# A decoder layer on one core: narrower score tiles, other head groups for the second attention, and three steps in another order

## The reference, cut to what matters

```
x = x + gla(layernorm(x))                 # stage a: gated linear attention, 16 heads, causal
x = x + xattn(layernorm(x), ctx)          # stage b: cross attention over 128 context rows
x = x + moe(layernorm(x))                 # 4 experts, top 2, capacity 512 tokens

gla:   S = S * exp(g) + k v^T ; o = q S   (per head, dk = 16, dv = 32)
       = for a block of 32 queries: scores = (q decayed)(k decayed)^T, masked, then times v
xattn: s = LN(q) LN(k)^T / sqrt(32); p = softmax(s); o = p v; out = o Wo
logits = layernorm(x) Wg                  # the router, 4 columns
```

## Time and profile before

| | us |
|---|---|
| runs | 1056.18, 1051.98, 1054.56 |
| median | 1054.56 |
| profiled execution, its own time | 1056.18 |
| its span, first to last instruction | 1054.4 |
| PE busy | 935.3 (89%) |
| DVE, POOL, ACT busy | 697.2, 493.9, 450.1 |

### The profile page before, as it was taken

The page is one execution under the profiler, slowest core; times in us unless marked ns, Lnnn a source line. Parts: engine busy times, 40 slices in busy tenths (PEclk is TensorE's granted clock), DMA queues, the critical chain, the costliest instruction groups (busy, mean ns, idle before and its releaser), DMA issues.

```text
span 1054.4 us, 19146 instructions
## 1 busy us (share of the span) xinstructions
PE 935.3 (89%) x7297; PEld 552.5 (52%) x7297; DVE 697.2 (66%) x1293; ACT 450.1 (43%) x754; POOL 493.9 (47%) x563
## 2 busy tenths in 40 slices
PE   3588999999999999999998763069999999999995
PEld 1445666667667666666665432024444444444342
DVE  6767787877887788878786435856555445446572
ACT  3444655665556655565565423112233323233210
POOL 1446676777777677767677520011070001003643
PEclk9788999999999999999999856569999999999998
DMA  9413000000000000000000005132335235235593
GB/s 288 132 51 127 4 17 17 4 17 17 14 17 3 17 14 17 2 17 17 14 2 14 12 11 197 52 119 81 118 85 182 96 119 161 82 117 171 175 245 129
DMA packets 40300, 78.39 MB, mean 74 GB/s; under 512 B 11378, under 2 KB 11650, under 8 KB 40258
## 3 DMA queue, kind: packets, MB, share of 16 engines
q1 hardware_dynamic: 35266, 63.13, 18.0%
q0 software_dynamic: 4992, 14.70, 5.1%
HBM read 64.16 MB, written 13.65 MB: 74 GB/s over the span
## 4 chain that ended last, share of the span: by engine, by line
PE 74%; DVE 7%; POOL 5%; issue 4%; DMA 4%; SPq 3%; ACT 2%; POOLq 0%; DVEq 0%; ACTq 0%
PE ps L1009 18%; PE ps L1010 17%; PE ps L1011 17%; PE ps L1015 6%; PE ps L1103 5%; PE ps L1195 3%; PE ps L1182 3%; POOL y_fetched L728 2%; PE ps L1206 2%; PE ps L1226 1%; POOL hrs L596 1%; DVE big L1678 1%; PE ps L1115 1%; SPq L473 1%; DMA y_fetched<-y_scratch,idx_get 1%
## 5 line engine op out<-in xcount | busy, mean ns | idle before, releaser
L596 POOL TENSOR_TENSOR hrs<-hve,neg_half 128x16 f32<-128x16 f32 x48 | 144.1, 3003 | 3.8
L982 ACT ACTIVATE big<-ps 128x512 f32<-128x512 f32 x64 | 38.2, 597 | 234.0 <-PE ps L1011 233.8
L1775 DVE TENSOR_SCALAR big<-big 128x512 f16<-128x512 f32 x64 | 27.7, 432 | 112.7 <-ACT big L982 112.7
L1009 PE MATMUL ps<-w2h,big 128*128 128x512 f16 x256 | 97.0, 379 | 2.7 <-DVE big L1367 2.7
L1009 PE MATMUL ps<-big,w1h 128*128 128x512 f16 x256 | 98.1, 383 | 1.4 <-DVE big L1367 1.4
L1010 PE MATMUL ps<-big,w1h 128*128 128x512 f16 x256 | 98.0, 383 | 0.0
L1011 PE MATMUL ps<-big,w1l 128*128 128x512 f16 x256 | 98.0, 383 | 0.0
L1011 PE MATMUL ps<-w2h,big 128*128 128x512 f16 x256 | 97.0, 379 | 0.0
L1010 PE MATMUL ps<-w2l,big 128*128 128x512 f16 x256 | 97.0, 379 | 0.0
L711 POOL DMA_INDIRECT big<-x_scratch,token_of x16 | 18.3, 1146 | 150.0 <-PE ps L1015 77.5
L728 POOL DMA_INDIRECT y_fetched<-y_scratch,idx_get x32 | 36.7, 1148 | 105.0 <-DMA y_scratch<-big 89.4
(11 more groups left out here) (305 smaller groups left out, 2498.8 us busy)
## 6 DMA issues: line engine op xcount, KB each, us to landing
wst<-in_w SPq DMA_DIRECT2D x28, 1024.0 KB, 5.2
x_scratch<-xn SPq DMA_DIRECT2D x16, 256.0 KB, 2.1
y_fetched<-in_w SPq DMA_DIRECT2D x4, 1024.0 KB, 13.7
out<-x_all SPq DMA_DIRECT2D x4, 1024.0 KB, 9.3
pr<-in_w_attn SPq DMA_DIRECT2D x3, 1024.0 KB, 9.1
x_all<-in_w_attn SPq DMA_DIRECT2D x3, 1024.0 KB, 11.7
x_all<-in_x SPq DMA_DIRECT2D x1, 3072.0 KB, 12.4
y_scratch<-big SPq DMA_DIRECT2D x3, 1024.0 KB, 6.1
```

Source lines behind the costliest of these rows:

```text
L596: pool.tensor_tensor(hrs[n][:, :], hve[n][:, :], neg_half[:, :], ALU.pow).then_inc(hdev[n], 1)
L982: act.activation(hg[f % 2], psum[f % 2][:, 512:1024], ACT.Gelu, scale=UN).then_inc(hg_r, 1)
L1009: nc.tensor.matmul(o, lh, rh, start=first, stop=False)
```

## The change

The score matmuls take exactly the width that their block needs. The four turns of b2 take two rows of heads and two columns each (`pv_heads`), so that turns 0 and 1 use only the half of the probabilities from round 0 and wait for that half alone; the values' matmuls follow the same grouping. On PE `a1_g` is one step, `b1_x` comes ahead of `b2_logits`. On ACT `x3_out` comes after the second layer norm's row and after `ctx_hi`, and `x2_hi` ahead of `logits_out`.

```diff
@@ ACT, body
                 on(s[1], kv_out)
-                on(s[3], x3_out)
                 on(s[1], row_norm, 1, xn2, xn2_r)
                 on(s[0], ctx_hi)
+                on(s[3], x3_out)
+                on(s[1], x2_hi)
                 on(s[3], logits_out)
-                on(s[1], x2_hi)
@@ PE, a2_scores
-                            w = max(KTW[i], 3 * BLK)
-                            o = psum[1][0:w, col:col + 256].rearrange(...)[:, :, i * BLK:(i + 1) * BLK]
-                            last = nc.tensor.matmul(o, kt[par][rw, c, KTO[i]:KTO[i] + w],
+                            o = psum[1][0:KTW[i], col:col + 256].rearrange(...)[:, :, i * BLK:(i + 1) * BLK]
+                            last = nc.tensor.matmul(o, kt[par][rw, c, KTO[i]:KTO[i] + KTW[i]],
                                                     qeo[par][rw, c * NBLK + i, :, :], start=True, stop=True)
@@ PE, b2
+            def pv_heads(g):
+                return [(2 * (g // 2) + i, 2 * (g % 2) + c) for c in range(2) for i in range(2)]
             def b2_turn(s, r):
-                for rnd in range(2):
-                    after(pe, pr_r[rnd], b)
+                after(pe, pr_r[r // 2], b)
...
-                for rr in range(4):
-                    last = nc.tensor.transpose(d0[:, rr * L:(rr + 1) * L], pg[:, rr * KC + r, :], ident[:, :])
+                for i, (rr, c) in enumerate(pv_heads(r)):
+                    last = nc.tensor.transpose(d0[:, i * L:(i + 1) * L], pg[:, rr * KC + c, :], ident[:, :])
             def b2_pv(s, r):
...
-                for rr in range(4):
-                    h = 4 * r + rr
-                    last = nc.tensor.matmul(d1[32 * rr:32 * rr + 32, r * L:(r + 1) * L], vx[par][:, h * DV:(h + 1) * DV],
-                                            pT[r % 2][:, rr, :], start=True, stop=True)
+                for i, (rr, c) in enumerate(pv_heads(r)):
+                    h = 4 * c + rr
+                    last = nc.tensor.matmul(d1[32 * rr:32 * rr + 32, c * L:(c + 1) * L], vx[par][:, h * DV:(h + 1) * DV],
+                                            pT[r % 2][:, i, :], start=True, stop=True)
@@ PE, body
                 on(s[3], b2_x3)
-                on(s[0], a1_g, range(KC // 2))
+                on(s[0], a1_g)
+                on(s[1], b1_x)
                 on(s[3], b2_logits)
-                on(s[0], a1_g, range(KC // 2, KC))
-                on(s[1], b1_x)
```

More of the change, by code:

```diff
@@ L1016, in turn, with rows @@
                 last.then_inc(done, 1)
-            def rows(ps, xh, xl, col, done, opens=True, ks=range(KC)):
-                for k in ks:
+            def rows(ps, xh, xl, col, done, opens=True):
+                for k in range(KC):
                     last = mm3(ps, xh[:, k, :], xl[:, k, :], wh[:, k, col:col + D], wl[:, k, col:col + D], opens and k == 0, k == KC - 1)
-                if k == KC - 1:
-                    last.then_inc(done, 1)
+                last.then_inc(done, 1)
             def second_kv():
@@ L1083, in a1_v, with a1_g @@
                 rows(a1, xth, xtl, C_V, v_ps)
-            def a1_g(s, ks):
+            def a1_g(s):
                 b, par, half = s
@@ L1088, in a1_g @@
                 after(pe, v_r, b)
-                rows(a1, xth, xtl, C_G, g_ps, ks=ks)
+                rows(a1, xth, xtl, C_G, g_ps)
             def a2_scores(s, rnd):
@@ L1100, in a2_scores @@
                             col = (r % 2) * 512 + c * 256
-                            w = max(KTW[i], 3 * BLK)
-                            o = psum[1][0:w, col:col + 256].rearrange("p (e t) -> p e t", e=2)[:, :, i * BLK:(i + 1) * BLK]
-                            last = nc.tensor.matmul(o, kt[par][rw, c, KTO[i]:KTO[i] + w],
+                            o = psum[1][0:KTW[i], col:col + 256].rearrange("p (e t) -> p e t", e=2)[:, :, i * BLK:(i + 1) * BLK]
+                            last = nc.tensor.matmul(o, kt[par][rw, c, KTO[i]:KTO[i] + KTW[i]],
                                                     qeo[par][rw, c * NBLK + i, :, :], start=True, stop=True)
```

## The result

The changed kernel takes 1095.56 us (median of 4 runs, 1094.20 to 1101.68) against 1054.94 us of the kernel before (4 runs, 1051.98 to 1056.18): a ratio of 1.0400, 95% interval 1.0355 to 1.0446, so 40.6 us slower. The forecast was 1086.6 us, 32 us slower, with a range up to 1098. Direction and range held; the size was 8.6 us short, and part of the time came by a way that the forecast doesn't name.

What follows compares the result with a forecast made beforehand. PE was taken to bound the loop, bodies 3 to 15. Widths 16.6, strips 12.8, half wait 0 and order 2.6 gave +32.0 us: 1086.6 us against the 1054.56 median; range for 8 in 10, 1072 to 1098.

Steps and rivals of the forecast that it cites:

- part 4: New order on PE and ACT: PE waits 0.3 us for x3T, 0.1 comes back; +2.6 us (0 to 5.2).
- the third rival: Ring of other engines bounds the loop, not PE; earlier x2h shortens bodies: -11, 1043.6 us; chance 0.03.
- the fourth: Rival for the whole kernel: what the change adds is hidden, time the same within 0.5%; chance 0.04.
- Part 1: Exact score widths: five more tile shape changes a round at 0.15 us, 0.23 saved; net +0.52 a round, +16.6 us.
- The first rival: Score rounds: changes between column widths within 32 rows don't drain; +8, 1062.6 us; chance 0.10.
- ten more waits put down to "issue" a body: Sign at the scores: PEld's count of waits put down to "issue" rises by some ten a body.
- Part 2: Values' matmuls in two strips instead of four: +0.21 us a step, four a sequence; +12.8 us (0 to 15).
- The changes of shape around it stay as they were: Value steps: assumed unchanged tile shape changes around each, so two more passes add +0.21 us to each step.
- The second rival: Value steps: four heads of `b2_pv` in two strips cost nothing more; +19.2, 1073.8 us; chance 0.10.
- Part 3: Turns waiting for half the probabilities: 3.8 us of slack in the loop, so nothing to gain; 0 us.
- just fits: Seam before the scores: `a1_g` ends at 317.54, xn2 at 317.36, so `b1_x` isn't delayed; 0.6 to spare before.
- is unchanged: PE between 314.95 and the scores at 318.88: same sum of instructions; only waits can change.

Runs made afterwards that it cites:

- the kernel with the blocks outside: Changed kernel with score loops turned round (query blocks outside, column halves inside), widths 128, 96, 64, 64: 1071.24 us, 1.0156 to the kernel before.
- the kernel with the strips: Kernel before with only the two-strip head groups and the wait for half of the probabilities: 1065.90 against 1060.44 us, 1.0055.
- the kernel with x3T first: Changed kernel with ACT's x3_out back ahead of the second layer norm's row, PE's order kept: 1091.47 us, 1.0343 to the kernel before.
- the first three experiments: Kernel before with one part each: exact score widths 1074.86 us, two-strip head groups 1065.90, new PE and ACT order 1068.27, against 1060.44.
- widths with strips: Changed kernel with the old order on PE and ACT, exact widths and head groups kept: 1078.47 against 1060.44 us, 1.0191.

## Why the forecast was right, and where it was not

**What bounds the kernel.** Right. The change of PE's busy time (+45 us) is about 2 us off the change of the span (+42.8), and the only wait for another engine that lengthened the body is the one for x3T, in part 4. By that the third rival falls (the ring of other engines): DVE's wait for x2h shrank from 2.91 to 2.11 us, and the body grew by the sum of PE's pieces. So does the fourth (hidden).

**Part 1, widths.** Right in mechanism, slightly long in size: 0.445 us a round instead of 0.52, because a change of shape from one width to another costs about 0.135 us and not 0.15. In 13 bodies that is 2.0 us less than forecast. The first rival (no drain between widths) is refuted by the round of 2.06 us. Shape by shape, PEld's loads did become shorter as forecast. Weight loads of the changed kernel from 150 to 187 (form, count, total us and mean ns of one, idle us before them):

```profile
L1101 PEld LDWEIGHTS ps<-qeo,kt 32*128 32x128 f32 x16 | 1.2, 182 | 0.4 <-issue 0.2
L1101 PEld LDWEIGHTS ps<-qeo,kt 32*96 32x96 f32 x16 | 1.0, 160 | 0.0
L1101 PEld LDWEIGHTS ps<-qeo,kt 32*64 32x64 f32 x16 | 0.8, 129 | 0.3
L1101 PEld LDWEIGHTS ps<-qeo,kt 32*32 32x32 f32 x16 | 0.6, 102 | 0.3
```

The last row gives back what was paid for, 160 down to 102 ns a load, while the round grew. One sign that the forecast gave did not come: ten more waits put down to "issue" a body. In the changed kernel the loads of L1101 in the loop have 12 such waits in 430 us, one a body. The price of the changes shows as idle time of which a good part has no releaser: in the page, the loads of the scores have 25.9 us of idle time before them where it was 16.6, of which "issue" is 13.7 and 14.6. Whoever looks for a change of shape within one line should read its round's length, not the waits.

The Trainium skill, "TensorEngine Tiling (Array Packing)", section Key Properties, says that switching the tiling mode drains the engine. These runs agree for a change of the columns alone within 32 rows, at 0.135 us a change. Its Overview's gain for a small free dimension of the left operand appears only where changes are few: -0.07 us a round in the kernel with the blocks outside, +0.445 in the changed one.

**Part 2, strips.** Right for three steps of four (0.56 us as forecast), wrong for the third, where "The changes of shape around it stay as they were" forgot that a neighbouring step in other strips can run beside it. 0.64 instead of 0.84 us a body, 2.6 us in 13 bodies. The second rival (free) is refuted.

**Part 3, the wait for half.** Nothing was seen that speaks against 0. It wasn't tried alone; the kernel with the strips has it in.

**Part 4, order.** The step that failed. PE's wait was sized at 0.3 us, of which 0.1 was to come back because 4-column passes drain sooner. The load waits 0.25 us for x3T and the body pays 0.28, so nothing came back; the kernel with x3T first has no such gain either (35.73 beside 35.74 in the old order). That b1_x "just fits" was right as to its cost: the loads' 0.19 us for xn2 lengthen nothing. The miss is 1 us in 13 bodies. The timeline of ACT at the seam of the changed kernel has the order of x3T after xn2 and cth as forecast (start us, us, what, idle before and releaser):

```profile
184.87 0.20 ACT L852 ACTIVATE act_pad<-rstd 128x1 f32<-128x1 f32 x1 [1.13 <-POOL shift_row L585]
...
185.69 0.37 ACT L872 ACTIVATE cth<-ctx 128x224 f16<-128x224 f32 x1
185.97 0.58 ACT L784 ACTIVATE x3T<-ps 128x512 f32<-128x512 f32 x1
```

And it left a term out. That the sum of PE's instructions between the end of b2_x3 and the scores "is unchanged" is true for the instructions and false for the clock at which they run: 19.5 of the 42.8 us. The clean row of the old loop, full clock in every slice of it, was taken as a property of the loop; it was one of its order.

**The sum.** Of the +32.0 us, 13 x 2.08 = 27.0 belonged to the 13 bodies and 5.0 to the stretches ahead and behind. Measured in the profiled execution: 23.4 at full clock, +2.1 ahead (2.1 were forecast) and -2.1 behind (2.9 were forecast), and 19.5 by the clock. So -3.6, -5.0 and +19.5 make the 10.9 us between +32.0 and the +42.8 of the spans (8.6 between the medians). That the range held is luck: errors of opposite sign and a wide upper end, not the working. With the 19.5 us of the clock added, the same working gives 1106 us, outside its range, and the profiled execution of the changed kernel took 1098.96 us where it said 1088.2.

## What is shown of the clock, and what stays open

Shown: the half clock in these 13 bodies goes with the order (0 stretches in the six kernels in which the logits stand apart from round 0, by the old order or by the new, and 2 to 12 in the five with b1_x, logits and round 0 in one piece), it does not need the exact widths, and it does not need the wait for x3T. With x3T first PE is counted as busy all the time ahead of it. On the whole more stretches come with a longer piece: 3.15 us 5, 3.22 us 2 and 6, 3.38 us 11, 3.67 us 12.

Open: whether it is the length of that piece or its make, since no kernel here has a piece over 2.59 us without the logits in it. The number also differs between two kernels with the same piece (2 and 6), so it isn't set by the piece alone, and each is read from one execution. In the kernel with the blocks outside, slow and full-clock bodies alternate from body 4 to body 9 with the same instructions in them. So the moment at which the piece comes may count as well, and with it the length of the body, which differs in these five kernels too; no run varies one of them alone. Nor does a run separate b1_x's transposes from the logits, or the logits from the wait for xn2 that comes with the new order.

Open too: why bodies 16 to 18 take 2.0 us less than before instead of 2.9 more. Their mean granted clock was 0.82 instead of 0.76, and in the nine experiments they take 80.5 to 84.6 us. The value steps of the last body weren't tried alone. The chip of the first three experiments and of widths with strips took 414 to 417 us for what comes behind body 18, the others 409 to 413, therefore only bodies and ratios on the same chip are compared.

## What to carry to other kernels

Count the changes of tile shape before cutting a matmul's width: here each costs 0.135 to 0.15 us, as much as streaming 150 or more weight columns, so matmuls of one shape belong together, and then narrow widths do pay (0.11 us of 34.22 a body here). Spread steps that hardly stream (transposes, passes of a few columns, narrow float32 matmuls) between streaming ones: put together, they made the clock fall to half though PE was counted as busy all the time, and a reordering that leaves the instructions alone cost 22.6 us of the 40.6 here (all but the 18.0 of widths with strips). Look at the granted clock body by body, not as a mean over the kernel, where 0.921 doesn't stand out.

## What was not expected of the hardware

Two steps of different kind and type, f32 passes in two strips and f16 passes of 16 columns in another, ran beside each other, so that a step that is 0.20 us longer cost 0.03. And a stretch at half clock cost on average the same 1.65 to 1.68 us in every kernel that had one (1.52 at the least in a single body), whatever their bodies held.
